# Exact LSTM steps on one core: the tanh of half 0's cell, and the product for half 0's h, each moved ahead of one operation of half 1

## The reference

```python
def step(carry, xp):
    h, c = carry
    gates = xp + h @ W_hh.T
    i, f, g, o = jnp.split(gates, 4, axis=-1)
    c = jax.nn.sigmoid(f) * c + jax.nn.sigmoid(i) * jnp.tanh(g)
    h = jax.nn.sigmoid(o) * jnp.tanh(c)
    return ((h, c), h)
...
logits = jnp.einsum('bth,lh->btl', lstm_out, W_lin) + b_lin
g = jax.lax.stop_gradient(jnp.argmax(logits, axis=-1).astype(lstm_out.dtype))[..., None]
w = g * lstm_out
inc = jnp.cumsum(w, axis=1)
prefix = inc - w
suffix = inc[:, -1:, :] - inc
return 2.0 * lstm_out + prefix * fw_att + suffix * bw_att
```

## Time and profile before

| | |
|---|---|
| median of 3 runs | 2087.95 us (2084.9 to 2088.72) |
| the profiled execution | 2089.04 us |
| its span, first to last instruction | 2086.9 us |
| busy: TensorE, VectorE, ScalarE, GpSimd | 1878.0, 1543.4, 1128.6, 230.3 us |
| mean granted share of TensorE's clock | 0.958 |

### The profile page before, as it was taken

How to read it: one execution, slowest core, us unless ns; L and a number is a source line. 1 busy time by engine, 2 the same in 40 slices (tenths; PEclk the granted TensorE clock), 3 DMA queues, 4 the chain that set the end, 5 groups by cost and what they waited for, 6 DMA issues and landing times.

```text
span 2086.9 us, 43187 instructions
## 1 busy us (share of the span) xinstructions
PE 1878.0 (90%) x13526; PEld 1606.4 (77%) x13526; DVE 1543.4 (74%) x4209; ACT 1128.6 (54%) x3147; POOL 230.3 (11%) x283
## 2 busy tenths in 40 slices
PE   5688998999999999999999899997789997999745
PEld 4467886888888888888888788885578997899733
DVE  7987887777777777777749877777866665666697
ACT  4475444444444444444434466667866665666527
POOL 3353001111011100110022200000000000000070
PEclk8899998999999999999999999999999998999975
DMA  4222321101010101110054022224543343333303
GB/s 133 89 79 75 98 95 41 36 28 35 25 35 28 35 28 33 31 32 30 30 161 119 26 98 118 118 106 146 171 129 109 129 129 101 100 129 129 110 0 123
DMA packets 95709, 170.50 MB, mean 82 GB/s; under 512 B 8213, under 2 KB 67369, under 8 KB 95296
## 3 DMA queue, kind: packets, MB, share of 16 engines
q1 hardware_dynamic: 66029, 84.75, 12.3%
q10 hardware_dynamic: 27248, 77.11, 11.4%
q0 software_dynamic: 2320, 7.26, 1.1%
HBM read 110.53 MB, written 58.56 MB: 81 GB/s over the span
## 4 chain that ended last, share of the span: by engine, by line
PE 63%; DVE 18%; ACT 9%; issue 7%; POOL 2%; DMA 1%; ACTq 0%; DVEq 0%; POOLq 0%
PE psum L678 27%; PE psum L832 16%; PE psum L673 7%; PE psum L789 4%; ACT scr L1139 2%; DVE scr L1528 2%; DVE scr L1736 2%; DVE bufB L1658 2%; ACT scr L1107 1%; PE psum L648 1%; DVE bufA L1872 1%; PE psum L622 1%; DVE bufB L1753 1%; DVE bufA L1864 1%; PE psum L799 1%
## 5 line engine op out<-in xcount | busy, mean ns | idle before, releaser
L1553 DVE TENSOR_TENSOR wx<-rs_buf 128x392 bf16<-128x392 bf16 (+1 forms) x1568 | 496.6, 387 | 163.5 <-PE psum L673 159.8
L678 PE MATMUL psum<-halves,counts 128*128 128x512 f32 x2401 | 599.7, 399 | 0.7 <-ACT counts L1045 0.7
L678 PEld LDWEIGHTS psum<-halves,counts 128*128 128x128 f32 x2401 | 437.5, 189 | 85.3 <-issue 0.9
L1045 ACT ACTIVATE counts<-psum 128x392 fp32r<-128x392 f32 x784 | 327.4, 505 | 273.2 <-PE psum L673 272.0
L832 PE MATMUL psum<-bufB,wx 128*128 128x125 f32 x3392 | 418.9, 282 | 23.1 <-ACT psum L1135 6.3
L832 PEld LDWEIGHTS psum<-bufB,wx 128*128 128x128 f32 x3392 | 399.1, 194 | 42.8 <-DVE bufB L1753 28.0
L673 PEld LDWEIGHTS psum<-wx 128*128 128x128 bf16 x3136 | 157.6, 98 | 39.3 <-issue 20.7
L673 PE MATMUL psum<-wx 128*128 128x98 bf16 x3136 | 183.9, 210 | 3.8 <-DVE wx L1553 2.7
L789 PE MATMUL psum<-bufA,wx 128*128 (+1 forms) x800 | 180.1, 376 | 3.1 <-POOL rs_buf L539 3.1
L1736 DVE TENSOR_TENSOR scr<-scr 128x125 f32<-128x125 f32 x280 | 81.1, 290 | 112.9 <-ACT scr L1139 106.7
L789 PEld LDWEIGHTS psum<-bufA,wx 128*128 128x128 f32 x800 | 146.7, 188 | 20.1 <-issue 3.3
(11 more groups left out here) (268 smaller groups left out, 2501.6 us busy)
## 6 DMA issues: line engine op xcount, KB each, us to landing
bufA<-gates_of_x ACTq DMA_DIRECT2D x136, 500.0 KB, 3.4
gates_of_x<-bufB SPq DMA_DIRECT2D x24, 1000.0 KB, 3.9
x_times_eps_plus_sums<-scr SPq DMA_DIRECT2D x50, 128.0 KB, 1.7
sums_by_feature<-scr SPq DMA_DIRECT2D x50, 128.0 KB, 1.9
scr<-x_times_eps_plus_sums SPq DMA_DIRECT2D x49, 128.0 KB, 2.0
wx<-in_x_dram SPq DMA_DIRECT2D x25, 250.0 KB
x_plus_mix<-wx SPq DMA_DIRECT2D x25, 250.0 KB, 4.5
bufB<-sums_by_feature SPq DMA_DIRECT2D x21, 250.0 KB, 3.0
```

The costliest lines, as they stand in the source:

```text
L678: return mm(psum[:, 3 + v, :], cnt[v][:, hi, :], xhl[:, hi, :, :].rearrange("p s d -> p (s d)"), start=(hi == 0), stop=(hi == NT - 1))
L1045: fn(cnt[v][:, :, c * u:c * (u + 1)], psum[:, CB[u % 4], 0:PER * KEYS].rearrange("p (c h) -> p h c", h=NT), ACT.Copy).then_inc(S["c_sb"], 1)
L1553: last = tt(to, tab2[:, 0:k_, :].unsqueeze(1).broadcast_to([P, PER // 2, k_, 2]), keysT[v][:, part_, g0:g0 + PER // 2, :].unsqueeze(2).bro ...
```

## The change

Two calls move up by one place, one on ScalarE and one on VectorE:

```diff
@@ -1152,8 +1152,8 @@
             def sweep_step(done, u):
                 half_if_out(done, u, 0)
                 half_go_out(done, u, 0)
+                half_cell(done, u, 0)
                 half_if_out(done, u, 1)
-                half_cell(done, u, 0)
                 half_go_out(done, u, 1)
                 half_cell(done, u, 1)
 
@@ -1756,8 +1756,8 @@
                 forget(done, u, 0)
                 enter_half(done, u, 0)
                 add_half(done, u, 0)
+                leave_half(done, t, 0)
                 forget(done, u, 1)
-                leave_half(done, t, 0)
                 enter_half(done, u, 1)
                 add_half(done, u, 1)
                 leave_half(done, t, 1)
```

## The result

The changed kernel took 2099.86 us (median of 5, 2099.21 to 2104.43) against 2087.95 us (median of 5, 2084.9 to 2088.72): a ratio of 1.0061, with a 95% interval of 1.0049 to 1.0072. In microseconds that is 11.9 more. The profiled execution took 2104.43 us against 2089.04, 15.4 more, of a span of 2102.3 us against 2086.9.

A forecast was written before the change was run, and what follows sets the result against it. The loop through h of half 1 was taken to bound each exact step, closing in 4.00 us. 106 steps times 0.145 us is 15.4 us, on the median 2087.95 a forecast of 2103.3 us, range 2099 to 2112.

The forecast's parts named there:

- the eleventh load: TensorE's first load in an exact step needing h of half 1; claimed to wait 0.08 us for it.
- two loops: Through each exact step: via h of half 0 (3.92 us alone) and via h of half 1 (4.00 us, closing last).
- The sum's term: Exact stage: each of 106 steps grows 0.145 us by ScalarE's new idling before half 0's tanh; 15.4 us in all.
- The bounds of 0.17 and 0.28: ScalarE's distance in us from half 0's tanh to half 1's sigmoid; bounds the total loss at 12.2 to 23.9 us.
- Covered moves: Exact steps: half 1's L1146 on ScalarE costs nothing; VectorE's h of half 0, 0.135 us earlier, buys nothing.
- the chain leave L1736: Sign in the changed profile: the chain of waits should leave L1736 and run through L1144 or L1742.
- loop B: From TensorE through half 1's sigmoid, half 0's tanh, half 1's g, c and h to the eleventh load; 4.00 us.
- Loop A governs: Rival, chance 0.06: h of half 0 sets each exact step, which shortens by 0.135 us; 14.3 us, to 2073.6.
- The whole 0.345 us goes through: Rival, chance 0.05: the full delay of half 1's sigmoid lengthens each exact step; 36.6 us, to 2124.5.

The follow-up runs named there:

- e2: Kernel before with only VectorE's move (h of half 0 ahead of half 1's f times c): step 4.200 us, 2109.49 us, ratio 1.0107.
- e3: Kernel before with two products by zeros added on TensorE ahead of the wait for h of half 1: step 4.149 us, 2100.60 us, ratio 1.0062.
- e6: Kernel before with half 0's tanh moved behind half 1's tanh of g, h of half 0 behind half 1's i times g: 4.277 us step, 2113.32 us.
- e3_zeros_after: Changed kernel with two products by zeros added on TensorE ahead of the wait for h of half 1: step 4.145 us, 2102.83 us.
- e1: Kernel before with only ScalarE's move (half 0's tanh ahead of half 1's sigmoid): step 4.343 us, 2122.72 us, ratio 1.0176.
- e4_c0_twice_before: Kernel before with the sum of half 0's c done twice on VectorE: step 4.076 us, 2094.40 us, ratio 1.0029.

## Why the prediction was right

- *Direction and mechanism.* It read the eleventh load at 1654.79 as a wait that no idle row shows, and from it two loops with the second closing last. e2, e3 and e6 show both loops, each by a run in which the other could not explain the step: 4.200, 4.149 and 4.277 us, forecast as 4.20, 4.13 and 4.26.
- *The sum's term.* Forecast 0.145 us a step, measured 0.141 (4.146 less 4.005). Its parts: L1748(0) to the tanh 0.32 (0.325 taken), tanh to L1139(1) 0.22 (0.20 taken), L1139(1) to L1144(1) 0.25 (0.28 taken). The last two miss by 0.02 and 0.03, with opposite signs; that they nearly cancel is luck. The bounds of 0.17 and 0.28 for the pair that the trace before didn't hold were wider than needed. The Trainium skill, ScalarE: Activation LUTs (Rules for kernel authors), budgets about 0.3 us and 0.83 ns an element for an activation whose bias is a pointer operand, an estimated 0.40 us for 125 columns. Such a one is L1107 of the earlier stage, and the trace of the kernel before agrees: 0.38 us each, with 0.25 us from one start to the next. The exact steps' activations pass no bias; those of 125 columns last 0.27 to 0.31 us and start 0.17 to 0.22 us apart, so that budget is no price for them.
- *The total.* Forecast 2103.3 us with a range of 2099 to 2112; measured 2099.86, within 1 us of its low end, and 2103.30 the second time; that the first fell inside owes something to luck. 106 steps times 0.141 is 14.9 us; the profiled executions differ by 15.4, and the medians by 11.9 and 16.7. The sigmoids of the exact stage run from 1530.8 to 1987.2 us in the changed kernel, 16.3 us longer than the 1531.8 to 1971.9 before, and begin 1.0 us earlier:

```profile
L1139 ACT ACTIVATE scr<-psum x212: 360/379/383, 1530.8 to 1987.2; 128x250 f32<-128x250 f32 x106
```

- *Covered moves.* L1146(1) hid, as said: it stands 0.28 behind L1144(1), with no wait for TensorE left, and nothing hangs on it. VectorE's early L1753(0) hid as well: TensorE's first load, 0.13 us less idle, ran into a longer wait (e3_zeros_after: 0.22 us of work there is free).
- *A detail that was wrong.* The prediction let the chain leave L1736. L1753(0) left it, but L1736(1) is still there: i times g of half 1 starts 0.22 behind it (1653.69 to 1653.91) and is held by it about as much as by g, a near tie that its own numbers (1657.615 and 1657.62) had shown. It also named loop B from TensorE to L1139(1); with the change that sigmoid is reached over c of half 0 and its tanh.
- *The rivals.* "Loop A governs" is refuted by the result, and by e2 on its own. The Trainium skill, Perfetto Trace Analysis (Optimization Strategy), says to find the gaps of the most contended engine and make what ends them start sooner. Here that did not help: TensorE's gap before a step's first load shrank from 0.29 to 0.16 us, a second one opened before the eleventh, and the kernel became slower. "The whole 0.345 us goes through" did happen, but in e1, where VectorE's half of the change is missing: 4.343 us.

## What to carry to other kernels

Before moving an operation earlier on an in-order engine, compare when its input arrives with when the input of the operation that it passes arrives: if its own comes later, the engine idles by the difference, and everything behind pays. In a recurrence, look for a second loop beside the one that the chain of waits prints: a wait shorter than the overlap of two instructions leaves no idle row, and only the distance between starts shows it (0.19 us between two loads that otherwise stand 0.11 apart). The cheapest test for room in a loop is a little work of no effect put into it, in both kernels: 0.22 us of it cost nothing in one and 0.14 us a step in the other.

## What the runs showed of the hardware

The places where a pass ends were not what I had counted on. There the chunks' ends are handed over, and TensorE has nothing to do. The kernel before, two stretches around its first such place (columns as in the earlier trace rows: length, busy time of TensorE, its loads, VectorE, ScalarE and GpSimd, granted clock, DMA share, GB/s):

```profile
1595.00:1598.00 3.00, 0.59 (x5) 0.41 (x4) 2.47 (x9) 1.25 (x4) 0.00 (x0) 1.00 0.33 92
1598.00:1601.00 3.00, 3.00 (x29) 3.00 (x28) 0.80 (x4) 1.15 (x5) 0.00 (x0) 1.00 0.20 79
```

and the changed kernel:

```profile
1596.00:1598.40 2.40, 0.22 (x2) 0.03 (x1) 1.92 (x8) 1.42 (x5) 0.00 (x0) 1.00 0.15 27
1598.40:1601.80 3.40, 3.03 (x14) 3.04 (x15) 0.72 (x2) 0.00 (x0) 0.00 (x0) 0.50 0.38 132
```

TensorE starts only 5 matmuls in 3.00 us before and 2 in 2.40 us after. In the first the granted clock stays at 1.00 (2.4 GHz) and 28 loads follow in 3.00 us; in the second it is at 0.50 (1.2 GHz) from 1598.4 to 1601.8 us and 15 loads take 3.40 us. The distance between the two steps is 6.24 us there before, and 7.83 with the change. It isn't the change's doing as such: the run e4_c0_twice_before, with the old order, has one place of each kind (6.31 and 7.94 us), and e1_act_only never falls at its first. The idle stretch before the next load is 2.66 us long at both places of e4_c0_twice_before, 2.59 at the one above that stays at 1.00 and 2.73 at the one that falls; so its length alone does not decide, and what does was not tried. Each fall costs about 1.6 us, and the changed kernel's profile has two of them. The distance over the stop before the comparison is 14.58 us there and 16.55 before, at a granted 0.50 for 10.2 and 13.6 us of it. Together these places are worth 1.3 us of the 16.3 by which the exact stage grew. They can be part of why equal steps gave totals a few us apart.
